# Attention scores computed with the keys on the partitions, two query tiles at a time, in two attention layers of a three-layer kernel

## The reference, cut to what matters

```python
def _cross_attention(q_in, kv_in, wq, bq, wk, bk, wv, bv, wo, bo, bias_k, bias_v):
    qh = (q_in @ wq + bq).reshape(b, q_len, H, K)
    kh = (kv_in @ wk + bk).reshape(b, t, H, K)
    vh = (kv_in @ wv + bv).reshape(b, t, H, K)
    kh = jnp.concatenate([kh, jnp.broadcast_to(bias_k, (b, 1, H, K))], axis=1)
    vh = jnp.concatenate([vh, jnp.broadcast_to(bias_v, (b, 1, H, K))], axis=1)
    logits = jnp.einsum('bqhk,bthk->bhqt', qh, kh) / scale
    weights = jax.nn.softmax(logits, axis=-1)
    ctx = jnp.einsum('bhqt,bthk->bqhk', weights, vh).reshape(b, q_len, H * K)
    return ctx @ wo + bo
```

## Time and profile before

| what | value |
|---|---|
| median of 3 runs | 1865.41 us (1865.3 to 1870.42) |
| the profiled execution | 1866.31 us |
| its span, first to last instruction | 1864.4 us |
| mean granted PE clock | 0.974 of 2.4 GHz |
| busy: PE, PEld, DVE, ACT, POOL | 92%, 78%, 65%, 55%, 21% |
| the chain that ended last, by engine | PE 71%, DVE 5%, ACT 2%, issue 2%, POOL 1% |

### The profile page before, as it was taken

The page is one execution under the profiler, slowest core; times in us unless marked ns, Lnnn a source line. Parts: engine busy times, 40 slices in busy tenths (PEclk is TensorE's granted clock), DMA queues, the critical chain, the costliest instruction groups (busy, mean ns, idle before and its releaser), DMA issues.

```text
span 1864.4 us, 31831 instructions
## 1 busy us (share of the span) xinstructions
PE 1711.7 (92%) x9942; PEld 1462.2 (78%) x9942; DVE 1217.4 (65%) x2487; ACT 1018.2 (55%) x1863; POOL 393.0 (21%) x320
## 2 busy tenths in 40 slices
PE   3698889897789999999999999799999999999997
PEld 2577777786568888888888877688888888888886
DVE  5577777777475666666665766766567566566664
ACT  2466666677344554554554556445455455555563
POOL 4456555542150000000000008410000000000063
PEclk8899999999789999999999999899999999999998
DMA  7767667766032101101101102420111011010021
GB/s 235 193 152 173 173 165 170 174 150 142 18 108 67 67 33 33 66 33 33 66 33 33 66 20 86 100 93 34 33 66 36 30 66 50 16 66 1 1 82 44
DMA packets 114097, 149.53 MB, mean 80 GB/s; under 512 B 25640, under 2 KB 99880, under 8 KB 114024
## 3 DMA queue, kind: packets, MB, share of 16 engines
q1 hardware_dynamic: 112680, 142.42, 27.8%
q10 hardware_dynamic: 1344, 6.19, 1.0%
HBM read 108.28 MB, written 3.42 MB: 60 GB/s over the span
## 4 chain that ended last, share of the span: by engine, by line
PE 71%; DVE 5%; ACT 2%; issue 2%; POOL 1%; DMA 0%; SPq 0%; DVEq 0%; ACTq 0%; POOLq 0%
PE ps L880 17%; PE ps L650 11%; PE ps L652 11%; PE ps L651 11%; PE ps L882 8%; PE ps L853 8%; PE ps L864 1%; DVE ar L1710 1%; DVE neg L1465 1%; ACT prob L1082 1%; PE ps L732 1%; DVE pt L1395 1%; PE ps L749 1%; DVE rr L1699 1%; DMA dk_raw<-in_bk 0%
## 5 line engine op out<-in xcount | busy, mean ns | idle before, releaser
L880 PE MATMUL ps<-cx,rr 128*128 128x512 f32 x1344 | 483.2, 402 | 2.2 <-issue 2.2
L1267 ACT ACTIVATE rr<-ps 128x512 fp32r<-128x512 f32 x336 | 200.5, 598 | 354.4 <-PE ps L853 352.7
L882 PE MATMUL ps<-cx,rr 128*128 128x256 f32 x1344 | 372.5, 277 | 0.0
L880 PEld LDWEIGHTS ps<-cx,rr 128*128 128x128 f32 x1344 | 252.2, 188 | 59.9 <-issue 6.8
L650 PE MATMUL ps<-ct,rr 128*128 128x500 f32 x672 | 279.7, 416 | 0.9 <-ACT ar L1238 0.6
L620 POOL TENSOR_SCALAR rr<-dvr,hsel 80x128 fp32r<-80x128 f32 x32 | 40.7, 1274 | 1093.1 <-DVE dvr L1605 993.4
L1586 DVE TENSOR_TENSOR rr<-ps,rr 128x512 fp32r<-128x512 f32 x336 | 231.7, 691 | 57.9 <-ACT rr L1267 41.3
L652 PE MATMUL ps<-ct,rr 128*128 128x500 f32 x672 | 261.1, 389 | 0.0
L651 PE MATMUL ps<-ct,rr 128*128 128x500 f32 x672 | 260.1, 387 | 0.0
L882 PEld LDWEIGHTS ps<-cx,rr 128*128 128x128 f32 x1344 | 253.2, 188 | 0.0
L1563 DVE TENSOR_REDUCE mx<-ps 128x1 f32<-128x500 f32 x336 | 227.5, 677 | 16.8 <-PE ps L652 9.5
(11 more groups left out here) (184 smaller groups left out, 3109.9 us busy)
## 6 DMA issues: line engine op xcount, KB each, us to landing
raw_t<-in_ctx_t SPq DMA_DIRECT2D x24, 1500.0 KB, 6.4
k<-khl SPq DMA_DIRECT2D x192, 187.5 KB
raw<-in_ctx SPq DMA_DIRECT2D x24, 1408.0 KB
raw<-stat_scratch ACTq DMA_DIRECT2D x7, 750.0 KB, 3.9
w_raw<-in_wq SPq DMA_DIRECT2D x32, 128.0 KB, 3.1
w_raw<-in_wk SPq DMA_DIRECT2D x32, 128.0 KB, 3.6
w_raw<-in_wv SPq DMA_DIRECT2D x32, 128.0 KB, 2.2
w_raw<-in_wo SPq DMA_DIRECT2D x32, 128.0 KB, 2.2
```

The source lines that it names most:

```text
L880: pe.matmul(ps[:, 6, :], pt[0:n, 0, c, :], cx[0:n, c, :], start=c == 0, stop=False, skip_group_check=True)
L882: mm = pe.matmul(ps[:, 6, 0:D], pt[0:n, 1, c, :], cx[0:n, c, 0:D], start=False, stop=c == CH - 1, skip_group_check=True)
L1267: act.activation(pt[:, 0, GRP * k:GRP * (k + 1), :], ps[:, 3 + k, :].rearrange("p (c q) -> p c q", q=P), ACT.Copy)\
```

## The change

In layers 2 and 3 the roles in the score product are exchanged. The context `ct` becomes the stationary operand, in 12 chunks of 125 keys (`KC`), and the queries the moving one. The scores come out with the keys on the partitions, which is what the weighted sum needs, so the 12 transposes of a tile go. Tiles are taken in units: three pairs of tiles (256 columns), and the seventh tile alone (128 columns). A unit's scores are 72 products in six PSUM banks, two chunks in each.

What replaces the row maximum is longer. DVE takes a running maximum over the six banks (`running_max`), PE turns it (`turn_max`), DVE reduces it and takes the minimum with the negated extra logit (`row_max`), PE spreads the negated maximum over the 125 partitions (`spread_max`), DVE copies it and adds it to each bank on the way to SBUF (`shift`), which also frees the bank. ACT takes exponentials in place and copies the high part; POOL subtracts the low part (`low_probs`). The row sum is now two columns of ones in `cx`, of which one is used; the weighted sum takes three products of 258, 256 and 258 columns a chunk in place of two. PE's order in a step is: all scores of the next unit (with the turn of the last output after the second bank), then the weighted sum of this unit, with `turn_max` and `spread_max` of the next in it.

Two thirds of each `cx` low split move from DVE to POOL; in `queries` ACT's `cx` splits come later. `raw` is loaded by one transfer a batch. In `outputs` the extra probabilities go out in two parts, 53 tiles before the last tile and 3 after it.

```diff
+KC = S // CH
+UNITS = (TILES + 1) // 2
+GROUPS = [CH // 2 if u < UNITS - 1 else CH // GRP for u in range(UNITS)]
+W = 2 * P
+CW = 2 * D + 2
...
+            def scores(i, b, u, j):
+                bc, q = (i - 1) * B + b, q_buf[u]
+                for k in (0, 1):
+                    v = slice(KC * (2 * j + k), KC * (2 * j + k + 1))
+                    out = ps[0:KC, j, W * k:W * k + (W if pair(u) else P)]
+                    for e in range(DH):
+                        mm = three(pe, out, ct[:, 0, e, v], ct[:, 1, e, v], q[:, 0, e, :], q[:, 1, e, :], e == 0,
+                                   e == DH - 1)
+                mm.then_inc(s["scores"], 1)
...
-            def transposes(r, t, g, k):
...
+            def weighted(i, b, u, t, chunks):
...
+                    pe.matmul(ps[:, bank, 0:D + 2], hi, cx[0:KC, c, 0:D + 2], start=c == 0, stop=False,
+                    pe.matmul(ps[:, bank, 0:D], hi, cx[0:KC, c, D + 2:CW], start=False, stop=False,
+                    mm = pe.matmul(ps[:, bank, 0:D + 2], lo, cx[0:KC, c, 0:D + 2], start=False, stop=c == CH - 1,
...
+                def step(b, u, last):        # PE, attention
...
+                    if not end:
+                        all_scores(i, nb, nu, turn_before)
...
+                    weighted(i, b, u, 0, range(0, 4))
+                    if not end:
+                        turn_max(i, nb, nu, o_before())
+                    weighted(i, b, u, 0, range(4, 9))
+                    if not end:
+                        spread_max(i, nb, nu)
+                    weighted(i, b, u, 0, range(9, CH))
+                    if pair(u):
+                        pe.wait_ge(s["m_ready"], units(i, nb, nu) + 1)
+                        weighted(i, b, u, 1, range(0, 6))
...
+                        turn_output(i, b, u, 0)
+                        weighted(i, b, u, 1, range(6, CH))
...
+                def step(b, u, last):        # ACT, attention
...
+                    if not (last and u >= UNITS - 2):
+                        split_q(i, *later)
+                    if not (zero(b) and u == 0):
+                        turn_output(i, *before, 1 if pair(before[1]) else 0)
...
+                    if not pair(u):
+                        split_cx(i, nb, 0)
+                        split_cx(i, nb, 1)
...
+                    extra_prob(i, nb, nu)
+                    exponentials(i, nb, nu, 0)
+                    for k in range(GROUPS[nu]):
+                        if k + 1 < GROUPS[nu]:
+                            exponentials(i, nb, nu, k + 1)
+                        if k == 0 and not pair(u):
+                            split_cx(i, nb, 2)
+                        if k == 0:
+                            scale_output(i, b, u, 0)
+                        high_probs(i, nb, nu, k)
+                        if k == min(2, GROUPS[nu] - 1) and pair(u):
+                            turn_output(i, b, u, 0)
+                        if k == min(4, GROUPS[nu] - 1) and pair(u):
+                            scale_output(i, b, u, 1)
...
+            def running_max(i, b, u, order=range(CH // 2), between=()):
...
+                for m, j in enumerate(order):
+                    dve.wait_ge(s["scores"], CH // 2 * n + m + 1)
...
+                        dve.wait_ge(s["run_step"], steps + m)
+                        ins = dve.tensor_tensor(top, src, top, ALU.max)
...
+                    if m < len(between):
+                        between[m]()
...
+                def step(b, u, last):        # DVE, attention
...
+                    if u == 0:
+                        split_cx(i, b)
+                    queries = () if last and u >= UNITS - 2 else (lambda: split_q(i, *later),)
+                    running_max(i, nb, nu, between=queries)
...
+                    row_max(i, nb, nu)
+                    shift(i, nb, nu, (None, lambda: sums(i, b, u, 0)))
...
+            def low_probs(i, b, u):          # POOL
...
+                    pool.tensor_tensor(group(p[:, 1, :, :], u, k), x, f(group(p[:, 0, :, :], u, k)), ALU.subtract)\
+                        .then_inc(s["p_lo"], 1)
```

More of the change, by code:

```diff
@@ L33 @@
 NS = 4
-PAD = P
-QBUF = [t % 2 if t < TILES - 1 else 2 for t in range(TILES)]
+KC = S // CH
+UNITS = (TILES + 1) // 2
+NU = B * UNITS
+GROUPS = [CH // 2 if u < UNITS - 1 else CH // GRP for u in range(UNITS)]
+G_AT = [sum(GROUPS[:u]) for u in range(UNITS + 1)]
+W = 2 * P
+CW = 2 * D + 2
+H_EARLY = (TILES - 3) * P // TQ
 PAIRS = H // 2
@@ new lines, in split_q, with extra_prob @@
+            def split_q(i, b, u):
+                q, src = q_buf[u], qo_tile(TILES * b + 2 * u, 2 if pair(u) else 1)
+                n = units(i, b, u)
+                if not isinstance(n, int) or n >= 2:
+                    wait_apart(act, s["scores"], CH // 2 * (n - 1))
+                act.activation(q[:, 0, :, :], src, ACT.Copy).then_inc(s["q_hi"], 1)
+            def extra_prob(i, b, u):
+                wait_apart(act, s["neg_ready"], units(i, b, u) + 1)
+                for t in range(2 if pair(u) else 1):
+                    g = TILES * b + 2 * u + t
+                    ins = act.activation(extra[:, bass.ds(g, 1)], lbq[:, bass.ds(g, 1)], ACT.Exp, bias=negm[:, t:t + 1])
+                ins.then_inc(s["ex_done"], 1)
@@ new lines, in shift @@
+            def shift(i, b, u, between=()):
+                n, count = units(i, b, u), 2 if pair(u) else 1
+                dve.wait_ge(s["max_b"], n + 1)
+                dve.tensor_copy(m_b[0:KC, 0:P * count], ps[0:KC, 7, 0:P * count]).then_inc(s["m_ready"], 1)
+                if not (zero(b) and u == 0):
+                    dve.wait_ge(s["p_lo"], groups(i, b, u))
+                dve.wait_ge(s["m_ready"], n + 1)
+                rows = W if pair(u) else P
+                m = m_b[0:KC, 0:rows].rearrange("p (c r) -> p c r", c=1).to_broadcast([KC, 2, rows])
+                for j in range(CH // 2):
+                    x = xp[0:KC, 2 * rows * j:2 * rows * (j + 1)].rearrange("p (c r) -> p c r", r=rows)
+                    src = ps[0:KC, j, :].rearrange("p (c r) -> p c r", c=2)[:, :, 0:rows]
+                    dve.tensor_tensor(x, src, m, ALU.add).then_inc(s["s_free"], 1)
+                    if j < len(between) and between[j] is not None:
+                        between[j]()
```

702 lines of the change are left out of this document (397 added, 305 removed).

## The result

The changed kernel takes 1982.92 us (1979.21 to 1984.45, 4 runs) against 1866.36 us (1865.3 to 1870.42, 4 runs), a ratio of 1.0617 [1.0595, 1.064]. That is 117 us slower; the forecast was 38 us slower, and its range ended at 1944 us. The profiled execution took 1984.45 us with a span of 1982.7; the spans differ by 118.3 us.

What follows compares the result with a forecast made beforehand. PE was taken to bound the attention loop. A batch of 67.4 + 3.2 + 0.8 = 71.4 us gave +40 over 16, layer ends -2: 1866.3 + 40 - 2 = 1904 us, eight-in-ten range 1862 to 1944.

Steps and rivals of the forecast that it cites:

- `queries`: In `queries`, DVE loses a 2.29 us split on which PE waited 2.50 us: -2.3 us a layer.
- `outputs`: In `outputs`, the 2.12 us wait for the extra probabilities goes, as most are sent earlier: -2.1 us a layer.
- The failed step: the clock: Rival: after the seventh tile's wait the clock falls too, in all 14 places: +30, 1934 us; chance 0.16.
- the walk: Step-by-step timing of the new chain in the loop: pairs hold with 0.4 us to spare, the seventh tile doesn't.
- The wait itself: After the seventh tile PE waits 3.2 us at `turn_max` for DVE's maxima, behind `split_q` and ACT.
- no-wait rival: In the batch loop PE stays full and only its work counts: 1840 us; chance 0.14.
- The sum over batches: Attention loops: a batch of 71.4 us, +2.5, taken 16 times: +40 us.
- The price of narrow products: Seventh tile's 128-column products cost 0.108 us each, bound by weight loads; 256 columns cost 0.118.
- The product sum: PE's products in a batch: -1.5 us, to 67.4 us; over 16 batches -24 us if PE never waits.
- Start of a layer: Nothing overlaps the chain from last maximum to first `shift`: about 3.4 us of PE idle, +3.4 a layer.
- End of a layer: End of each changed layer's attention loop: no separate wait or cost was given for it.
- The load of `raw`: Transfer of `raw` in each batch: one in place of two and a batch ahead, no cost given.

Runs made afterwards that it cites:

- experiments 2 and 3: Changed kernel with 13 or 27 extra products of 256 columns, result unread, ahead of `turn_max` in each batch's first unit: 1947.66 and 1946.09 us.
- Experiments 2, 3 and 9: The experiments 2 and 3, and the changed kernel with `turn_max` behind nine chunks and `spread_max` behind twelve in the waiting step: 1937.97 us.
- experiment 1: Changed kernel with DVE's low `split_q` moved from behind the first running maximum to behind the reduction of the maxima: 1892.00 us.
- Experiment 10: Changed kernel with low `split_q` behind the maxima, extra values prepared in each layer's first step, context load as 112 and 13 partitions: 1875.59 us.
- Experiment 5: Changed kernel with low `split_q` behind the maxima and the extra values prepared in each layer's first step: 1884.91 us.
- experiments 6 and 7: Changed kernel with the context load issued as 112 and 13 partitions (1973.94 us), or as two halves on 125 partitions (1980.85 us, one run).
- experiment 4: Changed kernel with the extra values' preparation moved from a layer's last batch to its first step: 1977.81 us.

## Why the prediction was wrong, by its own steps

The direction was right and the size was not: 1904 us was given, 1983 measured, outside the range. By the stages, against the forecast's +38 us:

| term | forecast | measured | miss |
|---|---|---|---|
| wait after the seventh tile, and smaller ones, products' sum | +40 | +48 | +8 |
| clock after that wait | a rival at 0.16, +30 | +39 | +39 |
| start and end of the attention loops | +6.8 | +30 | +23 |
| `queries` | -4.6 | -7.4 | -3 |
| `outputs` | -4.2 | -0.8 | +3 |
| first layer | 0 | +9.3 | +9 |
| rest | 0 | +0.8 | +1 |

The measured terms add up to 118.9 for the 118.3 of the spans. The first row is 14 batches at 75.1 less 2.8 and two at 68.9, each less 68.90; the rows are rounded. The third is start and loop together, less seven batches of 75.1 and one of 68.9 in the changed kernel and eight of 68.90 before.

- **The failed step: the clock.** The prediction named the fall of the clock and ranked it as a rival at 0.16, with the reason "dense products on both sides". It came true at every one of the 14 places, 6.8 us at half clock each time. The row that spoke for it was at hand: after 2.50 us of idle time the clock had fallen, and the walk itself gave 3.2. The reason against had no row behind it. Its price was low too: 2.2 us a time, worked out from 448-column products, against 2.8 (experiments 2 and 3). To the 3.5 us that the wait itself cost each time, 49 us in all, it added another 39. Experiments 2, 3 and 9 show that the wait is what does it, and not the narrow products before it.
- **The wait itself** was right in place, cause and size: 3.33 us against 3.2, DVE's maxima behind `split_q` behind ACT, with POOL holding the split (1.82 us against 0.69 in experiment 1; the forecast allowed 0.6 plus 1.3). The no-wait rival named the same remedy, "DVE's maxima not to stand behind `split_q`"; experiment 1 made it and the period fell to 68.86.
- **The sum over batches** counts the long wait 16 times, while the rival beside it has 14 places, and 14 there are: 14 x 3.2 and 16 x (0.8 - 1.5) are +34 and not +40. That the first row misses by only 8 us is thus partly luck: the two waits too many made up for a part of a wait priced 0.3 us too low and of small waits priced at half of what they are.
- **The price of narrow products** was right: from 699.75 to 702.38 us there are 24 steps in the changed kernel's timeline, 0.109 us each, against 0.108; and 256 columns are 0.118 to 0.12 apart, where 0.118 was taken. The some 81 ns of the Trainium skill, page "TensorE: Matmul & The Clock Gate", section "Back-to-back issue gap", which the prediction weighed against the rows, differ from this trace, and the trace decides.
- **The product sum** of 67.4 us isn't reached even without the wait. The best batch is 68.86: small waits of 0.15 to 0.25 us, half a microsecond in the seventh tile's step (14.1 for 13.6) and 0.4 in the next. The forecast had 0.8 for such waits, and 68.86 less 67.4 is 1.5. It leaves the change nothing to win when the long wait is gone.
- **Start of a layer.** +3.4 was only the idle time, and 3.2 us of that is there (0.88, 0.97 and 1.33). What was left out: two of the first unit's six banks are made inside `queries`, so four (48 products, 5.8 us) now stand open behind it, then a pair's scores (8.6 us) for a tile's (4.1) before the first weighted product, and the clock falls at 579. Some of it comes back as fewer scores later in the loop. Experiment 10, whose loop has no long wait behind its first step, still has starts of 20.4 us against 6.3.
- **End of a layer.** The preparation of the extra values was seen only as DVE work and not as something queued ahead of the last output's sum. It stood in the list 4.4 us, long beside POOL's subtractions: the same cast took 0.22 us before and 1.20 after. It cost a wait of 1.64 us, and 13.7 us at half clock follow it in each layer. Experiment 5, without it, is 7 us under experiment 1, though it waits 2.26 us in each layer's first step for the same work.
- **The load of `raw`** was costed at nothing, "one in place of two and a batch ahead". Its place was right and its shape was not looked at: 9 us in a layer that the diff doesn't touch (experiments 6 and 7).
- **`queries`** gave what was expected and a little more; in **`outputs`** the 2.12 us wait of the earlier trace rows went, but smaller ones stand in its place (0.46, 0.91 and 0.70 us at the second layer) and the stage is 0.1 and 0.7 us shorter instead of 2.1. Why not more was not tried.

What stays open: the experiments take 106 of the 117 us away. The 11 us by which experiment 10 stands over the kernel before lie in the starts (+14 us a layer) less `queries` (-3 to -5) and the loop (-2 to -6). Whether another order of a layer's first unit, the single tile first, would pay for it wasn't tried.

## What to carry to other kernels

When a walk ends with TensorE idle for longer than a wait after which the rows at hand show the clock fall, take the fall as the likely case and not as a rival: here it nearly doubled the price of the wait. Look in each in-order list for an instruction whose input is late and which nothing soon needs, in front of one that PE needs soon; moving it was worth 89 us here, and filling the wait only the clock's part. And read the partition count of every transfer that is reshaped: 125 partitions moved 1.5 MB on 5 of 16 engines and held back the loads of another layer.

## What the runs showed of the hardware that wasn't expected

- The clock at the same kind of place: after waits of 1.49 and 1.76 us the next 7 us ran at 1.00, after 3.33 us at 0.52 (1.2 GHz for most of it). In between one and the same place goes both ways. Windows of experiment 10, right behind the wait in the first step: 2.26 us of it in the second layer, 2.43 us in the third.

```profile
582.43:586.43 4.00, 4.00 (x22) 4.00 (x22) 1.48 (x3) 0.48 (x2) 0.00 (x0) 0.57 0.73 175
1255.71:1259.71 4.00, 4.00 (x34) 4.00 (x35) 2.68 (x6) 0.48 (x2) 0.00 (x0) 1.00 0.81 172
```

The longer wait left the clock alone. So did the 2.12 us of the kernel before, while 2.10 us in the third layer of experiment 4 was followed by a fall (0.64 over the next 4 us). And the 1.64 us at the end of a layer had 13.7 us at half clock behind it, where 1.76 us in the loop had none. The length of one wait alone doesn't tell. The wait at the end lies among products of 128 columns, and those at a layer's start (0.88, 0.97 and 1.33 us) close together; whether that is what made the clock fall there wasn't tried.
- At half clock the 128-column products are 0.21 us apart, against 0.109, and those of 256 columns 0.215, against 0.12: the whole pair of load and product slows, not only the moving of columns.
- The hold between DVE and POOL reached instructions that the prediction had not counted: a cast and a copy with one SBUF input each, 80 and 64 partitions by 128, took 1.20 and 1.21 us beside POOL's subtractions, where the cast took 0.22 us before. The sum of line 1806, which reads PSUM, took 0.16 us right behind them. The Trainium skill, page "SBUF — State Buffer", section "SBUF: two separate sides", counts DVE instructions in a two-port mode among those that exclude POOL, and a float32 copy from SBUF to SBUF as one of them; the cast and the copy agree with it. The prediction had used the other half of that rule alone.
- SP's issue of a 187.5 KB transfer took 9.1 us with the 1.5 MB transfer on five engines ahead of it in the same queue, and 0.6 us in the kernel before and with 112 and 13 partitions.
